# Attention on Trainium2: which PSUM banks hold score maxima, exponents and small transposes

## The chip, the cores and the metric

The kernel runs on one core of one Trainium2 chip. The metric is the device time of one execution, in microseconds (us). Smaller is better. Engines are TensorE (PE for its matmuls, PEld for its weight loads), VectorE (DVE), ScalarE (ACT), GpSimd (POOL) and SyncE (SP, which here only issues DMAs). TensorE writes its results to PSUM, which has eight banks of 512 float32 columns by 128 partitions.

## The reference, cut to what matters

Six residual layers run on 16 sequences of 512 rows by 128 columns; the change touches the second, grouped attention with 16 heads, 4 key/value heads (one "group" each) and a head size of 8:

```python
q = rope(x @ Wq); k = rope(x @ Wk); v = x @ Wv      # 16 heads, 4 kv heads, 8 columns each
att = einsum('bhqd,bhkd->bhqk', q, repeat(k, 4)) * 8 ** -0.5
att = softmax(where(causal, att, lowest))
x = x + einsum('bhqk,bhkd->bhqd', att, repeat(v, 4)) @ Wo
```

The other five layers (an MLP, the same MLP again, an expert layer, a scan layer, a second expert layer) are not touched.

## The kernel before, in words

`attention` (line 627) handles 16 sequences n times 4 groups g, 64 groups in all. Each group has four heads. For a group the kernel does this.

**Scores and maxima.** The queries times keys are computed once with queries on the partitions, to find each row's maximum. They come as six tiles k0 to k5 (`S_TILES`, line 618), each of two or four heads by 128 to 512 keys. `scores` (line 730) issues for each head of a tile a matmul (L739) and a matmul that adds the causal mask (L741). VectorE's `maxima` (line 946, reduction L950) reduces a tile and increments `s_read`. The tiles go through two double banks, `s_ps[0]` and `s_ps[1]`, by turns: tile k waits until tile k-1 of the count before it, that is the tile that used the same double bank two tiles earlier, has been read (line 736).

**Rows of maxima.** `max_rows` (line 770) transposes the group's maxima into the bank `misc`, `copy_rows` on ScalarE (line 841) copies them out, GpSimd splits them in two bfloat16 parts, and SP sends them to DRAM and back as extra rows of the queries.

**Exponents.** The scores are computed a second time, transposed and with the maximum already subtracted, as ten tiles x0 to x9 (`less_max`, line 744, matmuls L751). ScalarE takes the exponent of each (L862) and increments `x_read`. These tiles go through two banks `x_ps`, so tile i waits until tile i-2 has been read (line 748). GpSimd zeroes the masked triangle (L917).

**Weighing and output.** `weigh` (line 755, L766, 32 matmul records per group) multiplies the exponents with the values into `o_ps`. ScalarE copies it out every second group. Then the result is transposed in `misc` (`turn_output`, L247), normalised by VectorE (`normalise`, L958 and L962), transposed back in `misc` (`turn_normal`, L787), copied by ScalarE (`copy_normal`, L853), multiplied by Wo in `misc` (`project`, L794) and added to the residual by VectorE (`add_output`, L969). Steps g = 3 and g = 0 hold a `turn_output`, g = 1 a `turn_normal`, g = 2 a `project`.

**Order.** Everything is written out by hand, each engine working its own list in order. In `step` TensorE goes through the ten exponent tiles of group g; before some of them it puts a score tile of the group three ahead (`S_BEFORE`, line 620). The order in a step is: k0, x0, x1, k1, x2, weigh of the group before, k2, x3, rows, x4, k3, x5, x6, k4, x7, the transposes or the projection, k5, x8, x9. VectorE reduces k0 to k5 and then does its normalise or add. ScalarE does x0 to x9 with `copy_output` after x2, `copy_rows` after x4, `copy_normal` after x8. `first` computes scores and maxima of three groups before the first exponent tile; the last three groups have no score tiles left to put between. The semaphore pair `misc_full` and `misc_read` counts all uses of `misc`.

Of the kernel before, what the change touches and what calls it, by code (L numbers as in the profile page):

```python
# [5 lines left out]
F32 = mybir.dt.float32  # L6
# [612 lines left out]
NS = len(S_TILES)  # L619
S_BEFORE = {0: 0, 2: 1, 3: 2, 5: 3, 7: 4, 8: 5}  # L620
NG = NKV // 2
DEN = 2 * HD
# [4 lines left out]
def attention(nc, sem, h, xres, q_dram, k_dram, v_all):  # L627

    m_dram = nc.dram_tensor("row_max", [2, 2, NH * C, P], BF16, kind="Internal").ap()
    with ExitStack() as tmp:  # L630
# [14 lines left out]
        s_ps = [ps(f"s{j}", [P, 2 * T], F32) for j in range(2)]  # L645
        x_ps = [ps(f"x{j}", [P, T], F32) for j in range(2)]
        o_ps = ps("o", [P, T], F32)
        misc = ps("misc", [P, T], F32)
        qk_in = [[s(f"qk_in{u}{g}") for g in range(NKV)] for u in range(2)]
# [36 lines left out]
        with nc.Block() as block:  # L686
# [41 lines left out]
            @block.tensor  # L728
            def _(pe):
                def scores(n, u, r, g, k):  # L730

                    if k == 0:
                        pe.wait_ge(qk_in[u][g], r * 64 + 64)
                    c, heads, pitch = S_TILES[k]
                    w = (c + 1) * P
                    after(pe, s_read, (n * NKV + g) * NS + k - 1)
                    for x, j in enumerate(heads):
                        q0, at = (g * GH + j) * T + c * P, x * pitch
                        pe.matmul(s_ps[k % 2][:, at:at + w], qr[u][0:KQ, q0:q0 + P], kr[u][0:KQ, g * T:g * T + w],  # L739
                                  start=True, stop=False)  # L740
                        mm = pe.matmul(s_ps[k % 2][:, at + w - P:at + w], h["identb"][:], h["maskb"][:], start=False, stop=True)  # L741
                    mm.then_inc(s_full, 1)

                def less_max(n, u, r, g, i):

                    if i == 0:
                        pe.wait_ge(m_in[u][g], r * 16 + 16)
                    after(pe, x_read, (n * NKV + g) * NX + i - 1)
                    for c, j, at in X_TILES[i]:
                        q0 = (g * GH + j) * T  # L750
                        mm = pe.matmul(x_ps[i % 2][:, at:at + T - c * P], kr[u][0:KM, g * T + c * P:g * T + (c + 1) * P],  # L751
                                       qr[u][0:KM, q0 + c * P:q0 + T], start=True, stop=True)
                    mm.then_inc(x_full, 1)

                def weigh(n, u, g):

                    if g == 0:

                        pe.wait_ge(va_done, n + 1)
                    if g % 2 == 0:  # L760

                        after(pe, o_copied, n * NG + g // 2)
                    pe.wait_ge(p_masked, (n * NKV + g) * 5 + 5)
                    order = sorted((c, j, i, at) for i in range(NX) for c, j, at in X_TILES[i])
# [5 lines left out]
                def max_rows(n, u, r, g, at):  # L770

                    pe.wait_ge(s_read, (n * NKV + g + 1) * NS)
                    after(pe, misc_read, at)
                    pe.transpose(misc[0:GH * C, 0:P], negmax[u][:, g * GH:(g + 1) * GH, :].rearrange("p j c -> p (j c)"),
                                 h["ident"][:]).then_inc(misc_full, 1)

                def turn_output(n, p, at):

                    pe.wait_ge(o_copied, n * NG + p + 1)
                    pe.wait_ge(misc_read, at)  # L780
                    transpose_chunks(pe, misc, o_t[p], h["ident"]).then_inc(misc_full, 1)

                def turn_normal(at):

                    pe.wait_ge(misc_read, at)
                    for c in range(C):
                        mm = pe.transpose(misc[:, c * P:(c + 1) * P], o_n[:, c, :], h["ident"][:])  # L787
                    mm.then_inc(misc_full, 1)

                def project(at):  # L790

                    pe.wait_ge(misc_read, at)
                    for c in range(C):
                        mm = pe.matmul(misc[:, c * P:(c + 1) * P], o_nt[:, c * P:(c + 1) * P], h["wo"][:], start=True, stop=True)  # L794
                    mm.then_inc(misc_full, 1)

                def step(n, u, r):
                    for g in range(NKV):
                        ahead, ahead_rows = later(n, u, r, g, LA), later(n, u, r, g, LA - 1)
                        for i in range(NX):  # L800
                            if ahead is not None and i in S_BEFORE:
                                scores(*ahead, S_BEFORE[i])
                            less_max(n, u, r, g, i)
                            if i == WEIGH_AT and g:
                                weigh(n, u, g - 1)
                            elif i == WEIGH_AT and not is_first(n):
                                weigh(n - 1, 1 - u, NKV - 1)
                            if i == ROWS_AT and ahead_rows is not None:
                                max_rows(*ahead_rows, use(n, g, True))
                            if i == MISC_AT and g == 3:  # L810
                                turn_output(n, 0, use(n, g, False))
                            elif i == MISC_AT and not is_first(n):
                                if g == 0:
                                    turn_output(n - 1, 1, use(n, g, False))
                                elif g == 1:
                                    turn_normal(use(n, g, False))
                                else:
                                    project(use(n, g, False))

                def first():  # L820
                    for g in range(LA):
                        for k in range(NS):
                            scores(*FIRST, g, k)
                        if g:
                            max_rows(*FIRST, g - 1, g - 1)

                def flush():
                    n, u, r = LAST
                    done = use(n, NKV - 1, False) + 1
                    weigh(n, u, NKV - 1)  # L830
                    turn_output(n, 1, done)
                    turn_normal(done + 1)
                    project(done + 2)

                schedule(pe, first, step, flush)

            @block.scalar
            def _(act):
                a = nc.scalar

                def copy_rows(n, g, at):
                    act.wait_ge(misc_full, at + 1)

                    after(act, m2_done, n * NKV + g - 1)
                    a.activation(m_row[g % 2][:], misc[0:GH * C, 0:P], ACT.Copy).then_inc(misc_read, 1)

# [4 lines left out]
                def copy_normal(at):  # L851
                    act.wait_ge(misc_full, at + 1)
                    a.activation(o_nt[:], misc[:], ACT.Copy).then_inc(misc_read, 1)  # L853

                def step(n, u, r):
                    for g in range(NKV):
# [3 lines left out]
                        for i in range(NX):  # L860
                            act.wait_ge(x_full, (n * NKV + g) * NX + i + 1)
                            a.activation(p_sb[g % 2][:, i, :], x_ps[i % 2][:], ACT.Exp, scale=SCALE).then_inc(x_read, 1)  # L862
                            if i == WEIGH_AT and g == 0 and not is_first(n):
# [79 lines left out]
            def _(dve):  # L943
                v = nc.vector

                def maxima(n, u, r, g, k):
# [3 lines left out]
                    v.tensor_reduce(negmax[u][:, h0:h0 + len(heads), c],  # L950
                                    s_ps[k % 2][:, 0:len(heads) * pitch].rearrange("p (j w) -> p j w", w=pitch)[:, :, 0:w],
                                    AX.X, ALU.max, negate=True).then_inc(s_read, 1)

                def normalise(n, p, at):

                    dve.wait_ge(misc_full, at + 1)
                    o = misc[:].rearrange("p (c j e) -> p c j e", c=C, e=32)
                    v.reciprocal(rden[:], o[:, :, :, DEN:DEN + 2]).then_inc(o_rden, 1)  # L958
# [8 lines left out]
                def add_output(n, at):  # L967
                    dve.wait_ge(misc_full, at + 1)
                    v.tensor_tensor(xres[:, n, :], misc[:], xres[:, n, :], ALU.add).then_inc(misc_read, 1)  # L969
# [616 lines left out]
```

## Time and profile before

| | |
|---|---|
| median of 3 runs | 1865.32 us (1864.91 to 1867.68) |
| the profiled execution: its own time | 1864.19 us |
| the profiled execution: span of the profile | 1862.1 us |
| attention, first scores to the last add | 271 to 899 us of the span |
| its steady part | about 316 to 867 us |
| granted TensorE clock over the span | 0.92 |

The profiled execution is 1.1 us under the median, inside the spread of the runs; its span is 2.1 us shorter than its own time. A timeline row gives the start, the duration and the operation; equal neighbours are merged ("x4"), and a bracket tells the engine's idle time before the row and who ended it. Matmuls are pipelined: one that starts 0.22 us after another may still have a duration of 0.38 us, so what a matmul costs TensorE is the distance to the next start.

### The profile page before, as it was taken

The page shows a single profiled execution, that of the slowest core. Times are in us where ns is not written, and L with a number is a line of the kernel's source. Part 1 is how long each engine was busy: PE and PEld are TensorE (multiplying, and loading weights), DVE is VectorE, ACT ScalarE, POOL GpSimd, SP SyncE. Part 2 cuts the span into 40 slices and gives each one's busy share as a digit, 9 for nine tenths or more (in the row PEclk, how much of TensorE's full clock was granted, in tenths as well). Part 3 has the DMA queues.
Part 4 walks back from the last instruction along what each step waited for, and adds up shares of the span by engine and source line. Part 5 has one row for each costly group of instructions (what it writes and reads, how often), then busy time and mean ns, then how long its engine had stood idle before and what let it go on. Part 6 is the DMA issues. An engine that isn't in the chain of part 4 may idle for free. (4 is left out here: it accounts for less than half of the span.)

```text
span 1862.1 us, 39185 instructions
## 1 busy us (share of the span) xinstructions
PE 1572.6 (84%) x11698; PEld 1107.7 (59%) x11698; DVE 1359.8 (73%) x3422; ACT 1091.8 (59%) x2225; POOL 759.1 (41%) x1170
## 2 busy tenths in 40 slices
PE   4878739999999999998699439999977752999998
PEld 1444424555555555554355329999964541999997
DVE  4898746777777777774488668777768976787776
ACT  2444313666666666666466427787755531878876
POOL 1565542343333333333233356665402212666540
PEclk9989856999999999999899669999998865999999
DMA  5111231111111111110011301111000110121110
GB/s 136 31 38 51 60 103 38 43 43 42 42 42 44 44 42 41 41 30 3 1 34 34 113 17 38 39 34 30 24 1 23 34 34 13 39 60 46 46 45 23
DMA packets 72819, 76.39 MB, mean 41 GB/s; under 512 B 13040, under 2 KB 61488, under 8 KB 72752
## 3 DMA queue, kind: packets, MB, share of 16 engines
q1 hardware_dynamic: 64560, 58.77, 11.0%
q0 software_dynamic: 8192, 16.79, 3.1%
q8 instruction: 34, 0.56, 0.1%
q14 instruction: 33, 0.27, 0.0%
HBM read 51.40 MB, written 24.12 MB: 41 GB/s over the span
## 5 line engine op out<-in xcount | busy, mean ns | idle before, releaser
L950 DVE TENSOR_REDUCE at_negmax<-at_s_ps 128x2 f32<-128x1024 f32 (+3 forms) x384 | 393.2, 1045 | 170.7 <-PE at_s_ps L741 167.7
L862 ACT ACTIVATE at_p<-at_x_ps 128x512 f32<-128x512 f32 x640 | 353.2, 591 | 159.1 <-PE at_x_ps L751 152.2
L917 POOL TENSOR_SCALAR_AFFINE_SELECT at_p<-at_p 128x256 f32<-128x256 f32 (+1 forms) x448 | 189.9, 436 | 348.9 <-ACT at_p L862 348.9
L1174 POOL DMA_INDIRECT e_x_in<-xn,e_row_c x256 | 258.1, 1008 | 145.7 <-POOL e_row_c L1170 103.5
L739 PE MATMUL at_s_ps<-at_kr,at_qr 72*128 72x512 bf16 (+3 forms) x1024 | 253.1, 312 | 20.7 <-DMA at_kr<-k_parts 18.1
L751 PE MATMUL at_x_ps<-at_qr,at_kr 74*128 74x512 bf16 (+3 forms) x1024 | 235.5, 305 | 22.4 <-ACT at_p L862 12.7
L1295 DVE TENSOR_TENSOR e_hid_lo<-e_hid,e_hid_hi 128x512 fp32r<-128x512 f32 x256 | 177.3, 693 | 84.8 <-ACT e_hid_hi L1259 84.5
L741 PE MATMUL at_s_ps<-maskb,identb 128*128 128x128 bf16 x1024 | 202.2, 226 | 0.0
L1258 ACT ACTIVATE e_hid<-e_h_ps 128x512 f32<-128x512 f32 x256 | 155.2, 606 | 39.3 <-PE e_h_ps L1200 38.8
L766 PE MATMUL at_o_ps<-at_p,at_va 128*32 128x512 f32 (+3 forms) x2048 | 156.4, 448 | 1.6 <-POOL at_p L917 1.6
L1259 ACT ACTIVATE e_hid_hi<-e_h_ps 128x512 fp32r<-128x512 f32 x256 | 156.2, 610 | 0.0
L1200 PE MATMUL e_h_ps<-e_x_hi,w_hi 128*128 128x256 f32 x512 | 156.0, 305 | 0.0
L751 PEld LDWEIGHTS at_x_ps<-at_qr,at_kr 74*128 74x128 bf16 x1024 | 84.5, 98 | 114.4 <-ACT at_p L862 83.5
L739 PEld LDWEIGHTS at_s_ps<-at_kr,at_qr 72*128 72x128 bf16 x1024 | 102.9, 100 | 81.5 <-issue 21.0
L1200 PE MATMUL e_h_ps<-e_x_hi,w_lo 128*128 128x256 f32 x512 | 145.3, 284 | 0.0
L1200 PE MATMUL e_h_ps<-e_x_lo,w_hi 128*128 128x256 f32 x512 | 144.9, 283 | 0.0
L1210 PE MATMUL e_yt_ps<-e_hid_hi,w_lo 128*128 128x256 f32 x512 | 144.4, 282 | 0.0
L1210 PE MATMUL e_yt_ps<-e_hid_hi,w_hi 128*128 128x256 f32 x512 | 144.2, 282 | 0.0
L1210 PE MATMUL e_yt_ps<-e_hid_lo,w_hi 128*128 128x256 f32 x512 | 144.1, 281 | 0.0
L1251 ACT ACTIVATE e_x_hi<-e_t_ps 128x256 fp32r<-128x256 f32 x128 | 49.4, 386 | 140.5 <-PE e_t_ps L1189 139.6
L366 PE MATMUL m_xt_ps<-m_hid,w2d 128*64 128x512 f32 x512 | 123.0, 597 | 5.7 <-DVE m_hid L556 5.0
L766 PEld LDWEIGHTS at_o_ps<-at_p,at_va 128*32 128x32 f32 x2048 | 61.4, 112 | 96.0 <-issue 83.5
(184 smaller groups left out, 3514.1 us busy)
## 6 DMA issues: line engine op xcount, KB each, us to landing
at_qr<-q_parts SPq DMA_DIRECT2D x192, 96.0 KB
k_parts<-m_kparts SPq DMA_DIRECT2D x48, 96.0 KB
at_kr<-k_parts SPq DMA_DIRECT2D x64, 72.0 KB
xres<-in_x_dram SPq DMA_DIRECT2D x8, 512.0 KB, 7.3
xn<-m_n_xhat SPq DMA_DIRECT2D x16, 256.0 KB, 2.3
e_x_in<-xn,e_row_c POOLq DMA_INDIRECT x256, 2.5
xn<-sc_n_xhat SPq DMA_DIRECT2D x16, 256.0 KB, 2.3
out_dram<-xres SPq DMA_DIRECT2D x16, 256.0 KB, 2.3
```

The costliest lines, as they stand in the source:

```text
L739: pe.matmul(s_ps[k % 2][:, at:at + w], qr[u][0:KQ, q0:q0 + P], kr[u][0:KQ, g * T:g * T + w], start=True, stop=False)
L741: mm = pe.matmul(s_ps[k % 2][:, at + w - P:at + w], h["identb"][:], h["maskb"][:], start=False, stop=True)
L751: mm = pe.matmul(x_ps[i % 2][:, at:at + T - c * P], kr[u][0:KM, g * T + c * P:g * T + (c + 1) * P], qr[u][0:KM, q0 + c * P:q0 + T], start= ...
L766: mm = pe.matmul(o_ps[32 * j:32 * j + 32, c * P:T], va[u][:, c, g, :], p_sb[g % 2][:, i, at:at + T - c * P], start=(c == 0 and g % 2 == 0) ...
L862: a.activation(p_sb[g % 2][:, i, :], x_ps[i % 2][:], ACT.Exp, scale=SCALE).then_inc(x_read, 1)
L917: sel = gp.affine_select(out=part, in_=part, compare_op=ALU.is_ge, fill=0.0, base=0, pattern=[[0, n] for n in part.shape[1:-1]] + [[1, P]] ...
L950: v.tensor_reduce(negmax[u][:, h0:h0 + len(heads), c], s_ps[k % 2][:, 0:len(heads) * pitch].rearrange("p (j w) -> p j w", w=pitch)[:, :, 0:w],
L1174: nc.gpsimd.indirect_dma_start(out=x_in[k][u][:], out_offset=None, in_=xn_dram, in_offset=bass.IndirectOffsetOnAxis(ap=row_c[k][:, u:u + 1 ...
L1200: mm = pe.matmul(h_ps[half][:, f, :], w1[:, k, at:at + P], x[k % 2][:], start=(j == 0), stop=(j == len(pairs) - 1))
L1210: mm = pe.matmul(yt_ps[:], w2[:, k, f * D:(f + 1) * D], x[k % 2][:, f, :], start=(f == 0 and j == 0), stop=(f == FC - 1 and j == len(pairs ...
L1259: a.activation(hid_hi[k % 2][:, half * HC:(half + 1) * HC, :], h_ps[half][:], ACT.Gelu).then_inc(gelu_done, 1)
L1295: v.tensor_tensor(hid_lo[k % 2][:, chunks, :], hid[half][:], whole(hid_hi[k % 2][:, chunks, :]), ALU.subtract).then_inc(hl_done, 1)
```

## The change

`misc` goes away. Its bank becomes a third bank of `x_ps`, and tile x of the whole sequence (0 to 39) uses bank x mod 3. The small transposes and the projection go through the double banks of the maxima: the rows of maxima through the second one (`rows_ps`), the three others through the first (`turned`). The score tiles no longer take the double banks by turns but by the list `S_SLOT`. VectorE does its normalise or add ahead of the reduction of k5. In `first` the rows of maxima come after k2. The core of the diff (the helpers that read `misc` now read `turned` or `rows_ps`, and the calls pass the group ahead):

```diff
+S_SLOT = [0, 1, 0, 0, 1, 1]
+XB = 3
-        x_ps = [ps(f"x{j}", [P, T], F32) for j in range(2)]
+        x_ps = [ps(f"x{j}", [P, T], F32) for j in range(XB)]
-        misc = ps("misc", [P, T], F32)
+        turned, rows_ps = s_ps[0][:, 0:T], s_ps[1][0:GH * C, 0:P]
 ...
-                    after(pe, s_read, (n * NKV + g) * NS + k - 1)
+                    after(pe, s_read, (n * NKV + g) * NS + (-2, 0, 1, 3, 2, 5)[k])
+                    if rows is not None and k in (0, 4):
+                        after(pe, misc_read, rows + (1 if k == 4 else 0))
 ...
-                    after(pe, x_read, (n * NKV + g) * NX + i - 1)
+                    at = g * NX + i
+                    if at >= XB:
+                        pe.wait_ge(x_read, n * NKV * NX + at - XB + 1)
+                    else:
+                        after(pe, x_read, n * NKV * NX - (0, 2, 1)[at])
 ...
+                    if ahead is not None:                      # in max_rows
+                        pe.wait_ge(s_read, (ahead[0] * NKV + ahead[3]) * NS + 2)
 ...
+                def turned_free(at, ahead):                    # in the three others
+                    pe.wait_ge(misc_read, at)
+                    if ahead is not None:
+                        pe.wait_ge(s_read, (ahead[0] * NKV + ahead[3]) * NS + 4)
 ...
                 def first():                                   # TensorE
                     for g in range(LA):
                         for k in range(NS):
-                            scores(*FIRST, g, k)
-                        if g:
-                            max_rows(*FIRST, g - 1, g - 1)
+                            scores(*FIRST, g, k, g - 1 if g and k == 4 else None)
+                            if g and k == 2:
+                                max_rows(*FIRST, g - 1, g - 1, FIRST + (g,))
 ...
                 def step(n, u, r):                             # VectorE
-                            for k in range(NS):
+                            for k in range(NS - 1):
                                 maxima(*ahead, k)
                         if g == 3:
                             normalise(n, 0, use(n, g, False))
 ...
+                        if ahead is not None:
+                            maxima(*ahead, NS - 1)
```

## Rows read from the trace of the kernel before

**Rows 1.** Busy time by stretch: us, then PE, PEld, DVE, ACT, POOL, clock, DMA

```profile
316.45:867.00 550.55, 531.82 (x5110) 303.89 (x5110) 390.67 (x459) 354.78 (x702) 218.20 (x566) 1.00 0.13 39
```

**Rows 2.** The waits of 400 to 700 us: total, times, longest

```profile
PEld at_x_ps L751 <- ACT at_p L862: 41.9, 125, 0.9
```

**Rows 3.** Timeline of TensorE, one step with g = 2

```profile
610.88 0.38 PE L739 MATMUL at_s_ps<-at_kr,at_qr 72*128 72x512 bf16 x1
...
612.49 0.39 PE L751 MATMUL at_x_ps<-at_qr,at_kr 74*128 74x512 bf16 x1 [0.59 <-ACT at_p L862]
...
613.27 0.38 PE L751 MATMUL at_x_ps<-at_qr,at_kr 74*128 74x512 bf16 x1
...
615.87 0.34 PE L739 MATMUL at_s_ps<-at_kr,at_qr 72*128 72x384 bf16 x1
...
616.33 0.38 PE L751 MATMUL at_x_ps<-at_qr,at_kr 74*128 74x512 bf16 x1
...
616.88 0.33 PE L739 MATMUL at_s_ps<-at_kr,at_qr 72*128 72x384 bf16 x1
...
618.11 0.27 PE L739 MATMUL at_s_ps<-at_kr,at_qr 72*128 72x256 bf16 x1
...
619.96 0.22 PE L739 MATMUL at_s_ps<-at_kr,at_qr 72*128 72x128 bf16 x1
...
620.43 0.60 PE L751 MATMUL at_x_ps<-at_qr,at_kr 74*128 74x256 bf16 x4
620.87 0.38 PE L739 MATMUL at_s_ps<-at_kr,at_qr 72*128 72x512 bf16 x1
```

**Rows 4.** Timeline of TensorE, the step before it (g = 1)

```profile
601.88 0.38 PE L739 MATMUL at_s_ps<-at_kr,at_qr 72*128 72x512 bf16 x1
...
603.23 0.38 PE L739 MATMUL at_s_ps<-at_kr,at_qr 72*128 72x512 bf16 x1
...
608.63 0.27 PE L739 MATMUL at_s_ps<-at_kr,at_qr 72*128 72x256 bf16 x1
...
609.97 0.22 PE L739 MATMUL at_s_ps<-at_kr,at_qr 72*128 72x128 bf16 x1
```

**Rows 5.** Timeline of VectorE: k2 and k3, k4, an add, a normalise

```profile
616.53 1.96 DVE L950 TENSOR_REDUCE at_negmax<-at_s_ps 128x2 f32<-128x768 f32 x2 [1.83 <-PE at_s_ps L741]
618.99 1.23 DVE L950 TENSOR_REDUCE at_negmax<-at_s_ps 128x4 f32<-128x1024 f32 x1 [0.51 <-PE at_s_ps L741]
...
621.23 0.68 DVE L969 TENSOR_TENSOR xres<-at_misc_ps,xres 128x512 f32 x1
...
602.25 0.35 DVE L958 RECIPROCAL at_rden<-at_misc_ps 128x32 f32<-128x32 f32 x1
602.63 0.49 DVE L962 TENSOR_TENSOR at_o_n<-at_misc_ps,at_rden 128x128 f32<-128x128 f32 x2
```

**Rows 6.** Timeline of ScalarE and GpSimd around the same change of step

```profile
610.86 0.60 ACT L862 ACTIVATE at_p<-at_x_ps 128x512 f32<-128x512 f32 x1 [0.53 <-PE at_x_ps L751]
611.35 0.59 ACT L853 ACTIVATE at_o_nt<-at_misc_ps 128x512 f32<-128x512 f32 x1
611.83 1.68 ACT L862 ACTIVATE at_p<-at_x_ps 128x512 f32<-128x512 f32 x3
...
612.60 0.63 POOL L917 TENSOR_SCALAR_AFFINE_SELECT at_p<-at_p 128x512 f32<-128x512 f32 x1 [0.81 <-ACT at_p L862]
```

**Rows 7.** Timeline of the scores in `first`, at half clock

```profile
282.28 0.50 PE L739 MATMUL at_s_ps<-at_kr,at_qr 72*128 72x384 bf16 x1
...
283.36 0.96 DVE L950 TENSOR_REDUCE at_negmax<-at_s_ps 128x2 f32<-128x768 f32 x1 [0.17 <-PE at_s_ps L741]
```

**Rows 8.** The last groups: a wait with the weigh behind it, and one stretch

```profile
870.10 0.88 PE L751 MATMUL at_x_ps<-at_qr,at_kr 74*128 74x512 bf16 x2 [0.51 <-ACT at_p L862]
870.91 3.83 PE L766 MATMUL at_o_ps<-at_p,at_va 128*32 128x512 f32 x32
...
872.00:874.00 2.00, 2.00 (x20) 0.81 (x16) 0.00 (x0) 0.00 (x0) 0.00 (x0) 0.50 0.00 0
```

More of the change, by code:

```diff
@@ L729, in _, with scores @@
             def _(pe):
-                def scores(n, u, r, g, k):
+                def scores(n, u, r, g, k, rows):
                     if k == 0:
@@ L735, in scores @@
                     w = (c + 1) * P
-                    after(pe, s_read, (n * NKV + g) * NS + k - 1)
+                    after(pe, s_read, (n * NKV + g) * NS + (-2, 0, 1, 3, 2, 5)[k])
+                    if rows is not None and k in (0, 4):
+                        after(pe, misc_read, rows + (1 if k == 4 else 0))
                     for x, j in enumerate(heads):
                         q0, at = (g * GH + j) * T + c * P, x * pitch
-                        pe.matmul(s_ps[k % 2][:, at:at + w], qr[u][0:KQ, q0:q0 + P], kr[u][0:KQ, g * T:g * T + w],
+                        pe.matmul(s_ps[S_SLOT[k]][:, at:at + w], qr[u][0:KQ, q0:q0 + P], kr[u][0:KQ, g * T:g * T + w],
                                   start=True, stop=False)
-                        mm = pe.matmul(s_ps[k % 2][:, at + w - P:at + w], h["identb"][:], h["maskb"][:], start=False, stop=True)
+                        mm = pe.matmul(s_ps[S_SLOT[k]][:, at + w - P:at + w], h["identb"][:], h["maskb"][:], start=False, stop=True)
                     mm.then_inc(s_full, 1)
@@ L747, in less_max @@
                         pe.wait_ge(m_in[u][g], r * 16 + 16)
-                    after(pe, x_read, (n * NKV + g) * NX + i - 1)
+                    at = g * NX + i
[3 more added lines that the diff above has]
+                        after(pe, x_read, n * NKV * NX - (0, 2, 1)[at])
                     for c, j, at in X_TILES[i]:
                         q0 = (g * GH + j) * T
-                        mm = pe.matmul(x_ps[i % 2][:, at:at + T - c * P], kr[u][0:KM, g * T + c * P:g * T + (c + 1) * P],
+                        mm = pe.matmul(x_ps[(g * NX + i) % XB][:, at:at + T - c * P], kr[u][0:KM, g * T + c * P:g * T + (c + 1) * P],
                                        qr[u][0:KM, q0 + c * P:q0 + T], start=True, stop=True)
@@ L768, in weigh, with max_rows, turn_output, turn_normal @@
                     mm.then_inc(pv_done, 1)
-                def max_rows(n, u, r, g, at):
+                def max_rows(n, u, r, g, at, ahead):
                     pe.wait_ge(s_read, (n * NKV + g + 1) * NS)
+                    if ahead is not None:
+                        pe.wait_ge(s_read, (ahead[0] * NKV + ahead[3]) * NS + 2)
                     after(pe, misc_read, at)
-                    pe.transpose(misc[0:GH * C, 0:P], negmax[u][:, g * GH:(g + 1) * GH, :].rearrange("p j c -> p (j c)"),
+                    pe.transpose(rows_ps, negmax[u][:, g * GH:(g + 1) * GH, :].rearrange("p j c -> p (j c)"),
                                  h["ident"][:]).then_inc(misc_full, 1)
-                def turn_output(n, p, at):
+                def turned_free(at, ahead):
+                    pe.wait_ge(misc_read, at)
+                    if ahead is not None:
+                        pe.wait_ge(s_read, (ahead[0] * NKV + ahead[3]) * NS + 4)
+                def turn_output(n, p, at, ahead):
                     pe.wait_ge(o_copied, n * NG + p + 1)
[L780 to L785, printed above, removed]
+                    turned_free(at, ahead)
+                    transpose_chunks(pe, turned, o_t[p], h["ident"]).then_inc(misc_full, 1)
+                def turn_normal(at, ahead):
+                    turned_free(at, ahead)
                     for c in range(C):
-                        mm = pe.transpose(misc[:, c * P:(c + 1) * P], o_n[:, c, :], h["ident"][:])
+                        mm = pe.transpose(turned[:, c * P:(c + 1) * P], o_n[:, c, :], h["ident"][:])
                     mm.then_inc(misc_full, 1)
-                def project(at):
-                    pe.wait_ge(misc_read, at)
+                def project(at, ahead):
+                    turned_free(at, ahead)
                     for c in range(C):
-                        mm = pe.matmul(misc[:, c * P:(c + 1) * P], o_nt[:, c * P:(c + 1) * P], h["wo"][:], start=True, stop=True)
+                        mm = pe.matmul(turned[:, c * P:(c + 1) * P], o_nt[:, c * P:(c + 1) * P], h["wo"][:], start=True, stop=True)
                     mm.then_inc(misc_full, 1)
@@ L801, in step @@
                             if ahead is not None and i in S_BEFORE:
-                                scores(*ahead, S_BEFORE[i])
+                                scores(*ahead, S_BEFORE[i], use(n, g, True))
                             less_max(n, u, r, g, i)
@@ L808, in step @@
                             if i == ROWS_AT and ahead_rows is not None:
-                                max_rows(*ahead_rows, use(n, g, True))
+                                max_rows(*ahead_rows, use(n, g, True), ahead)
                             if i == MISC_AT and g == 3:
-                                turn_output(n, 0, use(n, g, False))
+                                turn_output(n, 0, use(n, g, False), ahead)
                             elif i == MISC_AT and not is_first(n):
                                 if g == 0:
-                                    turn_output(n - 1, 1, use(n, g, False))
+                                    turn_output(n - 1, 1, use(n, g, False), ahead)
                                 elif g == 1:
-                                    turn_normal(use(n, g, False))
+                                    turn_normal(use(n, g, False), ahead)
                                 else:
-                                    project(use(n, g, False))
+                                    project(use(n, g, False), ahead)
                 def first():
@@ L830, in flush @@
                     weigh(n, u, NKV - 1)
-                    turn_output(n, 1, done)
-                    turn_normal(done + 1)
-                    project(done + 2)
+                    turn_output(n, 1, done, None)
+                    turn_normal(done + 1, None)
+                    project(done + 2, None)
                 schedule(pe, first, step, flush)
@@ L844, in copy_rows @@
                     after(act, m2_done, n * NKV + g - 1)
-                    a.activation(m_row[g % 2][:], misc[0:GH * C, 0:P], ACT.Copy).then_inc(misc_read, 1)
+                    a.activation(m_row[g % 2][:], rows_ps, ACT.Copy).then_inc(misc_read, 1)
                 def copy_output(n, p):
@@ L852, in copy_normal @@
                     act.wait_ge(misc_full, at + 1)
-                    a.activation(o_nt[:], misc[:], ACT.Copy).then_inc(misc_read, 1)
+                    a.activation(o_nt[:], turned, ACT.Copy).then_inc(misc_read, 1)
                 def step(n, u, r):
@@ L861, in step @@
                             act.wait_ge(x_full, (n * NKV + g) * NX + i + 1)
-                            a.activation(p_sb[g % 2][:, i, :], x_ps[i % 2][:], ACT.Exp, scale=SCALE).then_inc(x_read, 1)
+                            a.activation(p_sb[g % 2][:, i, :], x_ps[(g * NX + i) % XB][:], ACT.Exp, scale=SCALE).then_inc(x_read, 1)
                             if i == WEIGH_AT and g == 0 and not is_first(n):
@@ L950, in maxima @@
                     v.tensor_reduce(negmax[u][:, h0:h0 + len(heads), c],
-                                    s_ps[k % 2][:, 0:len(heads) * pitch].rearrange("p (j w) -> p j w", w=pitch)[:, :, 0:w],
+                                    s_ps[S_SLOT[k]][:, 0:len(heads) * pitch].rearrange("p (j w) -> p j w", w=pitch)[:, :, 0:w],
                                     AX.X, ALU.max, negate=True).then_inc(s_read, 1)
@@ L956, in normalise @@
                     dve.wait_ge(misc_full, at + 1)
-                    o = misc[:].rearrange("p (c j e) -> p c j e", c=C, e=32)
+                    o = turned.rearrange("p (c j e) -> p c j e", c=C, e=32)
                     v.reciprocal(rden[:], o[:, :, :, DEN:DEN + 2]).then_inc(o_rden, 1)
@@ L968, in add_output @@
                     dve.wait_ge(misc_full, at + 1)
-                    v.tensor_tensor(xres[:, n, :], misc[:], xres[:, n, :], ALU.add).then_inc(misc_read, 1)
+                    v.tensor_tensor(xres[:, n, :], turned, xres[:, n, :], ALU.add).then_inc(misc_read, 1)
                 def step(n, u, r):
```

## The prediction, made before the changed kernel was run

> **What bounds the kernel now.** I read the busy time by stretch first. Over the steady part of attention, 550.55 us, TensorE is busy for 531.82 us (97%) at full clock, VectorE for 71% and ScalarE for 64% [rows 1]. TensorE bounds the layer, and only what holds TensorE up, or releases it, counts. Its busy time hides small holes, since durations overlap. So I read the waits next: between 400 and 700 us the weight loads of the exponent tiles waited for ScalarE for 41.9 us in 125 waits [rows 2]. This is what a third exponent bank can take away. Last I walked the timelines of one step on each engine, taking start to start as the cost.
>
> A matmul pair of two exponent tiles costs TensorE 0.44 us (620.43 to 620.87), so one tile costs 0.22; k0 or k1 costs 0.56 (612.49 plus 0.22 to 613.27), k2 or k3 0.46 (615.87 to 616.33) [rows 3]. From k0 to k1 there should then be 0.56 + 2 x 0.22 = 1.00 us. The step with g = 1 takes 1.35 (601.88 to 603.23) [rows 4], the one with g = 2 takes 0.83 too many (612.49 plus 0.22 less 610.88) [rows 3], because `copy_normal` sits between x8 and x9 on ScalarE. From k3 to k4 there should be 0.46 + 0.44 = 0.90 us, and there are 1.23 (616.88 to 618.11) [rows 3]. So the stalls that ScalarE causes are 0.35 + 0.33 = 0.68 us in an ordinary step and 0.83 + 0.33 = 1.16 us in a step with g = 2. A sequence of four steps has 3 x 0.68 + 1.16 = **3.20 us** of them. That is all that the third bank can give back, some 16 x 3.2 = 51 us.
>
> **The change, part by part.** Four waits are new or longer. The hand-over from a read to TensorE costs 0.06 us: x9's exponent ends at 611.83 + 0.60 = 612.43 [rows 6] and the released matmul starts at 612.49 [rows 3].
>
> *k3 after k2.* Both are in the first double bank, so k3 needs k2's reduction finished; before, it needed only k1's. VectorE starts k2 at 616.53, 0.66 us after its issue at 615.87, and one such reduction takes 0.96 us [rows 3, 5, 7]. k3 can start at 616.53 + 0.96 + 0.06 = 617.55. It started at 616.88, after x3, the rows and x4 [rows 3]. **0.67 us in each step, 2.68 in a sequence.** Queued behind it are x5, x6 and k4.
>
> *k5 after k4.* Both are in the second double bank. VectorE starts k4 at 618.99, 0.88 us after the issue at 618.11, and takes 1.23 us [rows 3, 5]. k5 can start 0.88 + 1.23 + 0.06 = 2.17 us after k4. It started 1.34 us after it (608.63 to 609.97) in an ordinary step [rows 4] and 1.85 us after it where the projection lies between [rows 3]. **0.83 x 3 + 0.32 = 2.81 us in a sequence.** Behind it stand x8, x9 and the next step's k0.
>
> *k0 after the reader of `turned`.* From k5 to the next k0 are 0.91 us (619.96 to 620.87) [rows 3]. With a normalise VectorE is done early enough: it now goes ahead of k5's reduction, starts as k4's ends, and takes about 0.9 us (602.25 to 603.12) [rows 5], while k5, x8 and x9 are issued. The add takes 0.68 us there [rows 5] and is hidden too, and k5's reduction, pushed back behind them, is needed only by k1. But `copy_normal` comes after x8, and x8 now comes after the delayed k5. From k5's start at 609.97 [rows 4] to the copy's end at 611.35 + 0.59 = 611.94 [rows 6] are 1.97 us, with the hand-over 2.03. **1.12 us, once in a sequence.**
>
> *x0 of a sequence after x39.* 40 tiles on three banks leave tile 39 and tile 0 in the same bank. x8's exponent starts 0.89 us after k5 (609.97 to 610.86) and a queued one 0.49 us after the one before (610.86 to 611.35) [rows 4, 6]. So x9's ends 0.89 + 0.49 + 0.60 = 1.98 us after k5, and x0 may start at 2.04. It would start 0.91 + 0.56 = 1.47 us after k5. **0.57 us, once in a sequence.**
>
> *Moved at no cost.* The rows of maxima and the transposes keep their instructions; the rows wait for k1's read, which ended during the weigh, and `turned` waits for k3's read, which ends 0.66 + 0.96 + 0.06 = 1.68 us after k3's start, against 0.46 + 0.44 + 0.69 + 0.22 = 1.8 us of issue ahead of it (k4's 0.69 is my estimate from its eight matmuls in these rows). This cover is thin. k4's wait for `copy_rows` is covered by the stall of k3. No DMA is added. Next late is the weigh: GpSimd's select for x9 ends at 613.23, 1.40 us after x9's exponent began [rows 6], and with the ScalarE stall gone TensorE arrives just about then; I count 0.05 us twice in a sequence, 0.1.
>
> *The third bank.* With the stalls above, each exponent has more time than now, so I let all 3.20 us go. Bounds: nothing to 3.20.
>
> Sum of a full sequence: 2.68 + 2.81 + 1.12 + 0.57 + 0.10 - 3.20 = **+4.08 us**. There are 14 such (n = 1 to 14), 57.1 us.
>
> *The ends.* In `first` the clock is half. k3's reduction starts 1.08 us after its scores (282.28 to 283.36) and VectorE idled 0.17 us for it [rows 7]. Now both k3 and k5 are issued only after the reduction before them, so each shows that whole 1.1 us. That is at most 2 us more per group and, as the idle time ahead of k0 shrinks, at least 1. I take 1.5, and 4.5 us for three groups (3 to 6). The first sequence is partly at half clock, where TensorE has no ScalarE stall to give back: I estimate 1 us per step, 4 us (3 to 6). The last sequence has k3 and k5 in one step only, about +1.4 us, and its other steps lack scores and gain from the third bank what ScalarE leaves; I take the two as equal, 0 (-2 to 2).
>
> Total 57.1 + 4.5 + 4 = 65.6 us. The profiled execution took 1864.2 us by its own time, so 1929.8; the median of the runs is 1.1 us above it. **I predict 1931 us**, with 1912 to 1940 as the forecast's own range (one new wait of the four missing or partly filled, or the bounds of the ends).
>
> **A rule against the change.** TensorE's clock can fall without a long pause. Near the end of attention it idled at most 0.51 us at a time, some of it in every microsecond, and in the middle of the next weigh the granted clock went to its lower level, 1.2 GHz: that weigh took 3.83 us against 2.4 (613.27 plus 0.22 to 615.87) [rows 3], and the stretch from 872 to 874 has 0.50 [rows 8]. In every step with g = 1 the stall ahead of k5 is followed, 0.9 us later, by the one of 1.12 us ahead of k0. The Trainium skill says, in "TensorE: Matmul & The Clock Gate", section "A second HAM failure mode: psum-queue depth-cycling", that small idle times between groups of matmuls, made by turning through the banks, can keep the clock going down and up. By that rule the sum above is too small; the trace agrees where the scores are missing, and shows full clock where they are present, with up to 0.83 us of stall in a row.
>
> **The rivals.**
>
> *The clock falls now and then.* For it: the stall ahead of k5 and the one ahead of k0 add up to 0.83 + 1.12 = 1.95 us at one change of step. Against it: TensorE still streams for more than four fifths of a step. One fall costs about the 1.5 us that the weigh above lost, and as much again for scores beside it, 3 us. In a third of the sequences this gives 15 us more, 1946; in each of them 48 more, 1979. Chance 0.20.
>
> *Faster: the new waits find VectorE ready.* The place is the hand-over from k2 to k3 and from k4 to k5. If these cost nothing, the third bank's 3.20 us less 0.57 and 1.12 would remain, 1.5 us a sequence: 1840. It decides when the new waits together are below 3.20 us in a sequence. Against it: k2's reduction runs from 616.53 to 617.49, across the point where k3 started, and k4's ends at 620.22, after k5's start at 619.96 even in the longest step [rows 3, 5]. Chance 0.03.
>
> *Half the loss.* Either the wait of k0 on `copy_normal` and that of x0 overlap with others, or k5's delay is absorbed because k0 and the weigh wait for GpSimd anyway: 1.5 to 2.5 us less in a sequence, 1895 to 1910. I see no such wait in the rows. Chance 0.10.
>
> *The change doesn't do what it says*, because ScalarE and not the bank is what the exponents wait for. Then the 3.20 us stay and all new waits come on top, 16 x 3.2 = 51 us more: 1982. Against it: ScalarE is only 64% busy [rows 1]. Chance 0.03.
>
> **How the numbers follow.** The forecast has 0.62, the rivals 0.20, 0.03, 0.10 and 0.03, and 0.02 is left for a time within 0.2% of the old one, about what a measurement of this kernel can tell from no change. The range goes from 1910 to 1962: below, it leaves out most of the half loss and the faster case, above, the frequent clock falls and the last rival. Slower by over 0.2% are all but the faster case and the rest: 0.95; same 0.02; faster 0.03.
>
> **What would show it.** In the profile after, a sequence should take about 41.1 us instead of 37.0 (9.99 us for the step with g = 2 and 9.00 for g = 1, 610.88 to 620.87 and 601.88 to 610.88, the other two taken like the latter) [rows 3, 4]. The waits should have a large new line of the score tiles (L739 of now) for VectorE, about 5.5 us in a sequence, in two kinds of 0.6 to 0.8 us, and the line of the exponent tiles for ScalarE should shrink to about one of half a microsecond per sequence. One wait of k0 for ScalarE's copy of about 1.1 us should stand in each g = 2 step. VectorE's idle time should grow, its busy time not. The granted clock should stay at 1.00 there; stretches at 0.50 would make the first rival right. I would be wrong if the score tiles' waits for VectorE were near zero.

## The result, and the profile after

The changed kernel took 1934.9 us (median of four), the one before 1866.5: a ratio of 1.039, 95% interval 1.031 to 1.048. In a second series it was 1934.0 against 1867.3, ratio 1.035 (1.034 to 1.037). It is slower by 68 us; I had predicted 1931. Three of its ten executions took 1959 to 1969 us, at a mean granted clock of 0.90 instead of 0.92, and none of the kernel before did so; the experiments come back to that.

The profiled execution took 1934.38 us, its span is 1932.3. The same stretch by stretch view as [rows 1]: TensorE is no longer busy for 97% of it but for 86%, at full clock.

```profile
316.45:867.00 550.55, 475.76 (x4612) 277.82 (x4605) 359.71 (x413) 318.59 (x630) 195.98 (x510) 1.00 0.13 37
```

The waits of 400 to 700 us of the changed kernel (L745 is the scores' matmul, L761 the exponents', L776 the weigh, L872 `copy_normal`). The wait of [rows 2] has shrunk from 41.9 us to 4.9, and the scores now wait for VectorE's reductions and for the copy. A PEld row and a PE row with the same count are one stall, seen by the weight load and by the matmul, and are not to be added:

```profile
PEld at_s_ps L745 <- DVE at_negmax L969: 45.5, 59, 0.9
...
PE at_s_ps L745 <- DVE at_negmax L969: 30.6, 59, 0.7
...
PEld at_s_ps L745 <- ACT at_o_nt L872: 9.9, 8, 1.2
PE at_s_ps L745 <- ACT at_o_nt L872: 7.7, 8, 1.0
...
PEld at_x_ps L761 <- ACT at_p L881: 4.9, 7, 0.7
PEld at_o_ps L776 <- POOL at_p L936: 4.7, 14, 0.3
```

The timeline of TensorE over one sequence answers to [rows 3, 4]. The brackets show the new stalls one by one:

```profile
602.45 0.38 PE L761 MATMUL at_x_ps<-at_qr,at_kr 74*128 74x512 bf16 x1
602.83 2.36 PE L776 MATMUL at_o_ps<-at_p,at_va 128*32 128x512 f32 x32
605.12 0.34 PE L745 MATMUL at_s_ps<-at_kr,at_qr 72*128 72x384 bf16 x1
...
606.79 0.34 PE L745 MATMUL at_s_ps<-at_kr,at_qr 72*128 72x384 bf16 x1 [0.50 <-DVE at_negmax L969]
...
607.69 0.27 PE L745 MATMUL at_s_ps<-at_kr,at_qr 72*128 72x256 bf16 x1
...
609.85 0.23 PE L745 MATMUL at_s_ps<-at_kr,at_qr 72*128 72x128 bf16 x1 [0.65 <-DVE at_negmax L969]
...
611.89 0.39 PE L745 MATMUL at_s_ps<-at_kr,at_qr 72*128 72x512 bf16 x1 [0.96 <-ACT at_o_nt L872]
...
612.88 0.38 PE L745 MATMUL at_s_ps<-at_kr,at_qr 72*128 72x512 bf16 x1
...
618.60 0.27 PE L745 MATMUL at_s_ps<-at_kr,at_qr 72*128 72x256 bf16 x1
...
620.77 0.23 PE L745 MATMUL at_s_ps<-at_kr,at_qr 72*128 72x128 bf16 x1 [0.15 <-DVE at_negmax L969]
...
630.62 0.23 PE L745 MATMUL at_s_ps<-at_kr,at_qr 72*128 72x128 bf16 x1 [0.66 <-DVE at_negmax L969]
...
632.66 0.60 PE L761 MATMUL at_x_ps<-at_qr,at_kr 74*128 74x512 bf16 x2 [0.41 <-ACT at_p L881]
```

From k2 to k3 are 1.67 us (605.12 to 606.79), before 1.01. From k4 to k5 are 2.16 (607.69 to 609.85) and, with the projection, 2.17 (618.60 to 620.77). From k5 to the next k0 are 2.04 us behind `copy_normal` (609.85 to 611.89), before 0.91. From k5 to x0 of the next sequence are 2.04 (630.62 to 632.66). From k0 to k1 are 0.99 us even behind the copy (611.89 to 612.88), where they were 1.83. These distances from start to start are what a stall costs; a bracket is smaller (0.50 us where k3 starts 0.66 later than before), since the matmuls ahead of it end later than the next could have started. In the same order VectorE's rows, which answer to [rows 5]:

```profile
605.78 0.96 DVE L969 TENSOR_REDUCE at_negmax<-at_s_ps 128x2 f32<-128x768 f32 x1 [1.76 <-PE at_s_ps L747]
...
608.57 1.23 DVE L969 TENSOR_REDUCE at_negmax<-at_s_ps 128x4 f32<-128x1024 f32 x1 [0.16 <-PE at_s_ps L747]
```

k2's ends at 606.74 and k3 starts at 606.79; k4's ends at 609.80 and k5 starts at 609.85. The hand-over is 0.05 us each time.

A sequence of four steps, measured from one `turn_normal` to that of the next sequence in TensorE's timeline, took 36.98 us before and takes 40.99 now, the same to 0.01 us in nearly all. A "fall" below is a stretch in which the granted clock goes from 1.00 to 0.50 (from 2.4 to 1.2 GHz) and back. This length is the best measure of the experiments, since it leaves out the ends of the layer:

| kernel | a sequence, us | time, us |
|---|---|---|
| before | 36.98 | 1866 to 1868 |
| changed | 40.99 | 1934 |
| n2_k5_late | 38.78 | 1897.5 |
| n3_k3_late | 40.12, with falls of the clock 41.7 and 43.4 | 1942.1 |
| n4_two_banks | 41.46, with falls 43.2 and 44.6 | 1955.0 |
| n5_half_k4 | 39.15, one with a fall 41.0 | 1905.7 |
| n6_half_k2 | 39.46 once, with falls 44.3 to 44.4 in nearly all others | 1965.3 |
| n7_old_dve_order | none without a fall: 45.6 with a short one, 47.3 to 50.6 with longer or two | 2037.9 |
| n8_halves | 35.22 | 1840.2 |
| n9_halves_shift | 35.05 | 1837.0 |
| n10_halves_two_banks | 37.47 | 1878.6 |

### The profile page after: what moved, and what is told of

The parts are those of the page before. It is cut to its first block and busy times, and to the rows that moved or that the text cites. A ratio compares the mean times of both kernels' runs of the same rounds, so it can differ in the third digit from the quotient of the medians.

```text
span 1932.3 us, 39373 instructions
## 1 busy us (share of the span) xinstructions
PE 1570.4 (81%) x11698; PEld 1114.3 (58%) x11698; DVE 1366.9 (71%) x3422; ACT 1090.5 (56%) x2225; POOL 757.2 (39%) x1170
## 5 line engine op out<-in xcount | busy, mean ns | idle before, releaser
L969 DVE TENSOR_REDUCE at_negmax<-at_s_ps 128x2 f32<-128x1024 f32 (+3 forms) x384 | 398.0, 1047 | 230.1 <-PE at_s_ps L747 229.8
L881 ACT ACTIVATE at_p<-at_x_ps 128x512 f32<-128x512 f32 x640 | 346.2, 596 | 225.3 <-PE at_x_ps L761 219.0
L745 PE MATMUL at_s_ps<-at_kr,at_qr 72*128 72x512 bf16 (+3 forms) x1024 | 254.0, 313 | 103.0 <-DVE at_negmax L969 71.1
L761 PE MATMUL at_x_ps<-at_qr,at_kr 74*128 74x512 bf16 (+3 forms) x1024 | 212.9, 302 | 8.7 <-ACT at_p L881 8.0
L745 PEld LDWEIGHTS at_s_ps<-at_kr,at_qr 72*128 72x128 bf16 x1024 | 101.3, 100 | 195.2 <-DVE at_negmax L969 106.9
L776 PE MATMUL at_o_ps<-at_p,at_va 128*32 128x512 f32 (+3 forms) x2048 | 155.2, 444 | 3.7 <-POOL at_p L936 3.3
L761 PEld LDWEIGHTS at_x_ps<-at_qr,at_kr 74*128 74x128 bf16 x1024 | 88.9, 98 | 57.7 <-ACT at_p L881 15.6
L776 PEld LDWEIGHTS at_o_ps<-at_p,at_va 128*32 128x32 f32 x2048 | 62.2, 111 | 99.0 <-issue 77.4
```

Of the source, the lines that this page charges most:

```text
L745: pe.matmul(s_ps[S_SLOT[k]][:, at:at + w], qr[u][0:KQ, q0:q0 + P], kr[u][0:KQ, g * T:g * T + w], start=True, stop=False)
L761: mm = pe.matmul(x_ps[(g * NX + i) % XB][:, at:at + T - c * P], kr[u][0:KM, g * T + c * P:g * T + (c + 1) * P], qr[u][0:KM, q0 + c * P:q0 ...
L881: a.activation(p_sb[g % 2][:, i, :], x_ps[(g * NX + i) % XB][:], ACT.Exp, scale=SCALE).then_inc(x_read, 1)
L969: v.tensor_reduce(negmax[u][:, h0:h0 + len(heads), c], s_ps[S_SLOT[k]][:, 0:len(heads) * pitch].rearrange("p (j w) -> p j w", w=pitch)[:, ...
```

## The experiments

**The changed kernel again**, beside the next three.

> The changed kernel as it is, to have its time beside the runs that follow, and because one of its first four executions took 1958.8 us at a mean granted clock of 0.902 where the others took 1934.4 to 1934.9 at 0.918. If the stalls of the change make the clock fall at times (the first rival of the prediction), executions near 1955 come up here too and none in the kernel before; a sequence otherwise takes 41.0 us. If it was a disturbance, nearly all are at 1934 to 1936.

1934.0 us, and two of six executions at 1967.2 and 1969.4, clock 0.903 and 0.900, where the others have 0.917 or 0.918. So the high one was not the only one. None of the three was profiled, so what fell in them is not seen, only in the runs below.

**k5 later.** `S_BEFORE` puts k5 ahead of x9.

```diff
-S_BEFORE = {0: 0, 2: 1, 3: 2, 5: 3, 7: 4, 8: 5}
+S_BEFORE = {0: 0, 2: 1, 3: 2, 5: 3, 7: 4, 9: 5}
```

> k5 is issued one exponent tile later (after x8). My theory, that TensorE waits for the end of k4's reduction and that the copy behind x8 is late only because x8 stands behind k5: the stall ahead of k5 shrinks by x8's 0.22 us in each step, the wait of k0 for the copy (1.12 us a sequence) goes nearly away, x0 at the start of a sequence waits about 0.3 instead of 0.57. A sequence falls from 41.0 to about 38.9 us, the time by 33 us to about 1902. Rival, that the stalls only move (the step is as long as the chain from exponents through GpSimd to the weigh allows): within 5 us of 1935.

1897.5 us and 38.78 us a sequence: my theory, 4 us on the fast side. One number in the order of issue gave back more than half of the loss, without a bank or an instruction changed. TensorE's wait ahead of k5 is 0.43 instead of 0.65 us, x8's 0.22 less, and k0's wait of 0.96 us for the copy is gone:

```profile
612.37 0.23 PE L745 MATMUL at_s_ps<-at_kr,at_qr 72*128 72x128 bf16 x1 [0.43 <-DVE at_negmax L969]
```

**k3 later**: in the changed kernel's `S_BEFORE`, `6: 3` for `5: 3`, with k5 back ahead of x8.

> k3 is issued one exponent tile later (after x5). My theory: x5's 0.22 us fills the stall ahead of k3, but the transposes and the projection, which need k3's tile read, get a stall of about 0.1 us in its place. Net 0.13 us in each step, about 8 us in all: about 1927. Rival, that the stall is not a wait for k2's reduction: no change or slower.

A sequence at full clock takes 40.12 us, 0.87 less where I expected 0.5: x5 fills 0.22 us of the stall in each of the four steps, and the new 0.1 us ahead of the transposes costs nothing, since k5 behind them waits for k4's reduction anyway (its wait is 0.51 us now, before 0.65). Yet the time is 1942.1, 15 us more than forecast. The timeline shows why: the clock fell eight times between 330 and 880 us, in some thirteen sequences. Two changes from g = 1 to g = 2, with k5, k0 and the weigh of each, and one stretch between:

```profile
530.49 0.23 PE L745 MATMUL at_s_ps<-at_kr,at_qr 72*128 72x128 bf16 x1 [0.51 <-DVE at_negmax L969]
...
532.52 0.39 PE L745 MATMUL at_s_ps<-at_kr,at_qr 72*128 72x512 bf16 x1 [0.96 <-ACT at_o_nt L872]
...
535.20 3.16 PE L776 MATMUL at_o_ps<-at_p,at_va 128*32 128x512 f32 x32
...
572.22 0.23 PE L745 MATMUL at_s_ps<-at_kr,at_qr 72*128 72x128 bf16 x1 [0.51 <-DVE at_negmax L969]
...
574.26 0.50 PE L745 MATMUL at_s_ps<-at_kr,at_qr 72*128 72x512 bf16 x1 [0.96 <-ACT at_o_nt L872]
...
577.67 4.10 PE L776 MATMUL at_o_ps<-at_p,at_va 128*32 128x512 f32 x32
...
534.00:536.00 2.00, 2.00 (x9) 0.60 (x11) 1.63 (x2) 1.18 (x3) 0.41 (x1) 0.50 0.33 94
```

Behind the two stalls of k5 and k0 the matmuls run at 1.2 GHz (0.50 of the full clock), and the weigh takes 3.16 or 4.10 us instead of 2.36. The first of these falls came 0.9 us after k0's start, at 533.4, the second at 574.4, 0.1 us after it. A stretch at the lower level lasts about 4 or about 7 us; a sequence with a short one takes 1.62 us more (41.74), with a long one 3.25 to 3.3 us more (43.4).

**Two exponent banks in the changed kernel.**

```diff
-XB = 3
+XB = 2
 ...
-                        after(pe, x_read, n * NKV * NX - (0, 2, 1)[at])
+                        after(pe, x_read, n * NKV * NX - (1, 0)[at])
```

> The maxima, transposes and projection as in the changed kernel, but the exponents go through two banks again; one bank is left unused. It shows what the third bank is worth once the new stalls are there. The prediction credited it with 3.20 us a sequence (some 50 us). If that holds in full, this run takes about 1985. By the walk of the queues it is less: while TensorE waits for VectorE, ScalarE catches up, so x6 waits for nothing with two banks, and only x1 at the change of step waits, about 0.35 us in three of four steps, while x0 of a sequence loses its wait of 0.57 us: about 0.5 us a sequence, so about 1943.

Sequences at full clock take 41.46 us, 0.47 more than with three banks: the walk's 0.5, not the prediction's 3.20. ScalarE's stall is down to about a third with two banks as well, 15.1 us where it was 41.9:

```profile
PEld at_x_ps L761 <- ACT at_p L881: 15.1, 49, 0.4
```

Between 330 and 880 us the clock fell six times, at the same change of step as above, at the end of k0's stall (451.9) or up to 2.1 us after it (411.0); such sequences take 43.2 or 44.6 us. That makes up the rest to 1955.0.

**Half of k4's reduction**, its maximum taken over half of the keys.

```diff
-                                    ...[:, :, 0:w],
+                                    ...[:, :, 0:w // 2 if k == 4 else w],
```

> Leaves out half of the keys in the maximum of tile k4 (the reduction reads 128 of each head's 256 columns), so the row maxima are not the true ones; everything else as in the changed kernel. If the stall ahead of k5 is the length of k4's reduction, the reduction falls from 1.23 to about 0.69 us, the stall by the same 0.54 us in three steps of a sequence and to nothing (0.32 less) in the step with the projection: 1.9 us a sequence, 41.0 to 39.1, about 1905 us, and no fall of the clock, since the two stalls at the change from g = 1 to 2 then add up to 1.4 us and not 1.9. If something else holds k5 (the hand-over, the weight loads): over 1925.

1905.7 us, 39.15 a sequence: both as expected, and the reduction is 0.69 us long. What I had expected of the clock is missed: in the profiled execution it fell once where scores are present, at 833.2, 0.9 us after a k0 that had waited 1.05 us for the copy, while k5 ahead of it had no stall that the view marks. So the longer of the two stalls is enough for a fall at times.

```profile
604.76 0.69 DVE L969 TENSOR_REDUCE at_negmax<-at_s_ps 128x4 f32<-128x512 f32 x1 [0.16 <-PE at_s_ps L747]
...
834.00:835.00 1.00, 1.00 (x5) 0.22 (x2) 0.60 (x2) 0.43 (x1) 0.41 (x1) 0.50 0.61 205
```

**Half of k2's reduction**, the same for k == 2.

> Leaves out half of the keys in the maximum of tile k2 (192 of 384 columns of each head). If the stall ahead of k3 is the length of k2's reduction, it shrinks by about 0.4 us in every step: 1.6 us a sequence, 41.0 to 39.4, 1909 us where the clock holds. The stalls ahead of k5 and k0 stay, so the clock may fall at the change from g = 1 to 2, 3.3 us each time: up to 1950 then, with stretches at half clock in the trace. If the stall ahead of k3 has another cause: 1933 or more.

The one sequence at full clock takes 39.46 us, as expected for the stall ahead of k3. Nearly all others take 44.3 to 44.4: here the clock falls in every one of them, twice in each, also behind the smaller stalls of k5 and x0 (0.66 and 0.34 us), where I had reckoned with one fall. A short and a long fall at n3's prices, 1.62 + 3.3 us, make up the 4.9 us. The kernel does less work than the changed one and takes 31 us more. k5, x0 and the weigh at such a change of sequence:

```profile
601.09 0.23 PE L745 MATMUL at_s_ps<-at_kr,at_qr 72*128 72x128 bf16 x1 [0.66 <-DVE at_negmax L969]
603.12 0.61 PE L761 MATMUL at_x_ps<-at_qr,at_kr 74*128 74x512 bf16 x2 [0.34 <-ACT at_p L881]
604.98 3.43 PE L776 MATMUL at_o_ps<-at_p,at_va 128*32 128x512 f32 x32
```

**VectorE's old order**, k5's reduction ahead of the normalise or the add.

```diff
-                            for k in range(NS - 1):
+                            for k in range(NS):
                                 maxima(*ahead, k)
 ...
-                        if ahead is not None:
-                            maxima(*ahead, NS - 1)
```

> The changed kernel with VectorE's old order: k5's reduction ahead of the normalise or the add. The prediction said that k0 finds `turned` read in time only because the normalise goes ahead of k5's reduction. If so, k0 now waits for the normalise about 1.3 us in two steps of a sequence and 1.1 us for the add in one, and the wait of x0 for x9 is hidden behind it: 3.1 us a sequence more, 41.0 to 44.1, 1982 us where the clock holds and up to 2030 where it falls once or twice in a sequence. Rival, that the order on VectorE does not matter since TensorE waits for k4's reduction anyway: 1934.

2037.9 us, 8 above the expected highest. The mechanism holds: k0 waits for the normalise. The shortest sequence takes 45.6 us against the 44.1 expected, and all later ones more, but none of those measured is free of falls; from 400 to 700 us the mean granted clock is 0.91. The shortest has one fall of 4 us (397.5 to 401.5), the next, 47.27 us, one of 7, and the one after it, 50.46 us, two of 7. Less n3's 1.62 and 3.25 us for each, this leaves 44.0 us in all three: an estimate, and it meets the 44.1 expected of the waits. What was too small is the share of the clock.

```profile
603.14 0.39 PE L745 MATMUL at_s_ps<-at_kr,at_qr 72*128 72x512 bf16 x1 [1.14 <-DVE at_o_n L981]
...
399.00:400.00 1.00, 1.00 (x8) 0.30 (x12) 0.81 (x1) 0.60 (x1) 0.15 (x1) 0.50 0.14 44
```

**The third bank without the new waits.** The free bank is still found, but each score tile keeps the distance of before.

```diff
-S_SLOT = [0, 1, 0, 0, 1, 1]
+S_SLOT = [0, 1, 0, 1, 0, 1]
 ...
-        turned, rows_ps = s_ps[0][:, 0:T], s_ps[1][0:GH * C, 0:P]
+        turned, rows_ps = s_ps[1][:, T:2 * T], s_ps[1][0:GH * C, 0:P]
 ...
-                    after(pe, s_read, (n * NKV + g) * NS + (-2, 0, 1, 3, 2, 5)[k])
-                    if rows is not None and k in (0, 4):
-                        after(pe, misc_read, rows + (1 if k == 4 else 0))
+                    after(pe, s_read, (n * NKV + g) * NS + (-1, 0, 1, 2, 3, 4)[k])
+                    if rows is not None and k in (1, 3):
+                        after(pe, misc_read, rows + (1 if k == 3 else 0))
 ...
-WEIGH_AT, ROWS_AT, MISC_AT = 2, 3, 7
+WEIGH_AT, ROWS_AT, MISC_AT = 2, 2, 7
 ...
-                            if i == ROWS_AT + 1 and ahead_rows is not None:    # ScalarE
+                            if i == ROWS_AT and ahead_rows is not None:
```

> The third exponent bank without the new waits. The score tiles alternate between the double banks as in the kernel before; the transposes and the projection go into the second half of the second double bank, which k5, only 512 columns wide, leaves free; the rows of maxima go into its first half right after the weigh, and are copied ahead of x3. My theory: k3 and k5 wait for nothing, k0 neither; k1 waits for the normalise and k5's reduction, 0.3 us in two steps, and 0.1 us for the copy in one; x0 of a sequence keeps its wait of 0.57 us; the weigh waits 0.05 us for GpSimd. A sequence takes 35.0 us against 37.0 before: about 1835 us. Rival, by what the two-bank run showed (the third bank worth 0.5 us a sequence): if ScalarE's stalls were not the bank's doing but come back at the weigh or at k1, a sequence takes 36.5 or more, 1858 or above.

1840.2 us against 1867.4, ratio 0.986 (0.984 to 0.988), 35.22 us a sequence. It beats both kernels; the time is 5 us above the expected.

**The same with the banks shifted** from tile 33 on.

```diff
+X_BANK = [(t + (2 if t >= 33 else 0)) % XB for t in range(NKV * NX)]
 ...
```

> The same, and the exponent banks are counted on by two from tile 33 of a sequence, so that tile 0 of the next takes the bank of tile 37 instead of that of tile 39. My theory: the wait of x0 for x9's exponent goes, but k1's wait of 0.3 us in that step shows in its place: 0.3 us a sequence, 4 us less than without the shift. Rival: the weigh behind it waits for GpSimd all the same, and nothing changes.

1837.0 us, ratio 0.984 (0.982 to 0.985), 35.05 a sequence: 0.17 less per sequence, about half of the expected. The times of single executions overlap with those of n8_halves, so this rests on the length of the sequence. TensorE is busy for 98% (491.89 of 503.55 us), and what is left is the weigh's wait for GpSimd and k1's for VectorE:

```profile
316.45:820.00 503.55, 491.89 (x4938) 299.76 (x4940) 376.19 (x445) 337.93 (x678) 212.09 (x551) 1.00 0.15 43
...
PEld at_o_ps L778 <- POOL at_p L938: 8.1, 16, 0.7
...
PE at_s_ps L747 <- DVE at_negmax L971: 4.1, 18, 0.2
```

**The halves version with two exponent banks.**

> The halves version (small transposes in the free half of the second double bank, no wait of k3 or k5) with two exponent banks instead of three. If the third bank makes the gain of that version, this one loses it and is back at the kernel before: 37.0 to 37.3 us a sequence, 1864 to 1873 us, with the weight loads of the exponent tiles waiting for ScalarE some 40 us between 400 and 700 us. Rival, that the moved rows and transposes made the gain: about 1840.

1878.6 us, ratio 1.006 (1.004 to 1.007), 37.47 us a sequence, 0.5 more than the kernel before. So the rest of that change (the moved rows and transposes, the new order on VectorE) costs a little, and the third bank gives 37.47 - 35.22 = 2.25 us a sequence here, against 0.47 in the changed kernel. ScalarE's stalls are back in full, 45.4 us where n8_halves (second row) has 6.7:

```profile
PEld at_x_ps L761 <- ACT at_p L881: 45.4, 125, 0.9
...
PEld at_x_ps L761 <- ACT at_p L881: 6.7, 9, 0.7
```

## Why the prediction was right, point by point

**The sum.** Predicted +4.08 us a sequence, measured 40.99 - 36.98 = 4.01. By terms, predicted and measured: k3 after k2 0.67 and 1.67 - 1.01 = 0.66; k5 after k4 0.83 and 2.16 - 1.34 = 0.82, with the projection 0.32 and 2.17 - 1.85 = 0.32; k0 after the copy 1.12 and 2.04 - 0.91 = 1.13; x0 of a sequence 0.57 and 2.04 - 1.47 = 0.57; the weigh's wait for GpSimd 0.05 and 602.83 less 602.45 less 0.31 = 0.07 (0.31 us from x2 to the weigh where it does not wait, 613.44 to 613.75). The half reductions, the later k5 and VectorE's old order each moved their own term, which shows the cause and not only the place.

**The ends.** The first `turn_normal` that TensorE reaches in the second sequence comes 12.0 us later than before (350.67 and 362.64), of which 2.4 us are already there when the first reduction starts (272.37 and 274.78), so before anything that the change touches. Of the other 9.6 us, 4.9 lie in `first` (from the first scores to the first exponent tile 294.63 - 271.08 = 23.55 us before and 301.97 - 273.49 = 28.48 now), where 4.5 were predicted. The remaining 4.6 hold the first sequence, predicted at 4, and the part of the second that lies ahead of that point, which I have not separated. From the first reduction to the last add attention takes 690.8 + 0.7 us and took 625.8 + 0.7: 65.1 us more, predicted 65.6. The remaining 5 us of the spans' 70.2 are 2.4 us ahead of attention and 2.7 behind it; I have no cause for them.

**What was credited wrongly.** The term of 3.20 us had the right size, and its reason, that with the stalls "each exponent has more time than now", was right too. But it was booked to the third bank, and this was wrong, with no effect on the sum. In the changed kernel the third bank is worth 0.47 us a sequence. The rest of the 3.20 goes with two banks as well, because TensorE now stands still for VectorE, and ScalarE catches up in that time. Where TensorE doesn't stand still the bank is worth 2.25.

**The clock.** I gave the first rival 0.20 as an addition to the forecast. The profiled execution of the changed kernel has the clock at 1.00 there, so the forecast holds for it and for seven executions of ten. But the rival is real: in variants with the same stalls at the change from g = 1 to g = 2 the clock falls behind them, in about every second sequence (n3_k3_late, n4_two_banks) or in nearly every one (n6_half_k2), at 1.6 to 3.3 us each (I had said 3); with the stall of k5 gone, in n5_half_k4, it fell once. The prediction read 0.51 us as the longest idle time ahead of the fall near the end of attention; some 9 us further back, at 861.47, there was one of 0.56. The rule of the Trainium skill, "TensorE: Matmul & The Clock Gate", section "A second HAM failure mode: psum-queue depth-cycling", that short idle times between groups of matmuls can make the clock go down and up, agrees with these traces: eight falls in n3_k3_late, behind idle pieces of 0.51 and 0.96 us. That it also explains the three executions at 1959 to 1969 us fits their clock of 0.90, but isn't shown. In the run that is without the copy's wait, n2_k5_late, and in n10_halves_two_banks no stretch between 330 and 865 us was at the lower level, nor in n8_halves and n9_halves_shift between 330 and 858.

**The rivals that fell.** Faster: the reductions were not ready. Half the loss: no stall overlapped another but those I had overlapped in the walk. "ScalarE and not the bank is what the exponents wait for": where TensorE isn't held up otherwise, their wait is 45.4 us with two banks (n10_halves_two_banks) and 6.7 with three (n8_halves).

## What to carry to other kernels

When a buffer is won by letting other tiles share theirs, write down for each tile which read it now waits for and how much TensorE work lies between. A double buffer whose turn comes twice in a row is a single buffer: its next writer stands still from the first matmul of the tile before to the end of that tile's read, here 1.67 or 2.16 us, less the work between (1.01 or 1.34 us). Look first for the half of a buffer that its smallest tile leaves free. The worth of a further bank can't be read from the waits it removes alone, because a new stall anywhere on the same engine removes them too.

## What the runs showed of the hardware that I had not expected

The clock does not need a long pause to fall: with idle pieces of 0.51 and 0.96 us and about 1.1 us of matmuls between them (n3_k3_late, 530.49 to 531.56) it went from 2.4 to 1.2 GHz, in n6_half_k2 with 0.66 and 0.34 us, and in n5_half_k4 behind one piece of 1.05 us. These pieces alone don't settle it: the changed kernel, with 0.65 and 0.96 us at the same place, had no fall there in either of its two profiled executions, and I can't say from these runs what decides. So a kernel that does less (n6_half_k2, 1965.3 us) can take longer than one that does more (1934.0).
